# A decoder layer in fp32: the attention's output projection as three fp32r products, and another order of the last batch's work

## The chip, the cores and the metric

The kernel runs on one core of a Trainium2 chip. The metric is the device time of one execution in microseconds. It is taken as the median of several runs.

## What is computed

Four batches (B = 4) of 256 tokens with 256 channels go through one layer of three parts. Each part ends in a residual and a layer norm. Cut to what matters:

```python
q, k, v = (x @ Wq), (x @ Wk), (x @ Wv)             # 16 heads of 128; q and k RMS-normed
attn = softmax(q @ k.T / sqrt(128) - slope_h * dist, causal)
y = rmsnorm(attn @ v) * subln_w
x = layernorm(x + y.reshape(B, T, 2048) @ Wproj)   # the output projection, 2048 -> 256
e = (ctx @ xWq.T + bq) @ (ctx @ xWk.T + bk).T
x = layernorm(x + x @ softmax(e))                   # mixes the 256 channels
xq = quantise(x, per token, 127 steps); gate, up, down weights ternary
h = sigmoid(xq @ gate.T) * (xq @ up.T)              # 1024 wide, quantised again per token
x = layernorm(x + quantise(h) @ down.T)
```

All of it is fp32, apart from the last part, whose quantised integers are exact in bf16. x, Wq, Wk and Wv are each split into a rounded part of type fp32r ("hi") and the rest of it, fp32r too ("lo"). A product of two such numbers is summed from three matmuls: hi by hi, hi by lo, and lo by hi.

## The kernel before, in words

The program is written engine by engine, with semaphores set by hand, and each engine does its instructions in the order written. A batch has 16 heads, so there are 64 heads. One loop of 68 steps is a pipeline of depth 4 over them. In step n the PE queue (lines 565 to 585) holds, in this order:

- `qkv(n, 0)` (line 504): token tile 0 of head n, six fp32r matmuls of 384 columns
- `turn_qk(n-1)` (line 514): four fp32 transposes; `turn_p(n-2)` (line 521): three
- the first side slot; then `qkv(n, 1)`
- `scores(n-1)` (lines 526, 527) and `values(n-2)` (lines 533 to 535), in fp32
- `project(n-4)` (line 546): for each of the two token tiles one fp32 matmul of `yT` by `wp[:, h]`, 256 columns wide, summed over the 16 heads in bank 7
- `turn_y(n-3)` (line 554): two transposes; then the second side slot

A side slot (`slots`, lines 49 to 79) may hold a job of the rest of the layer: the cross attention of the same batch, or the second and third part of the layer for the batch before. All such jobs write PSUM bank 6.

The other engines in step n:

- ScalarE (lines 724 to 770): two exponentials of head n-2 (731, 732), `yT` of head n-4 from PSUM to SBUF with a scale (737), the squares and the copy of v for tile 0 (709, 713), the copies of q, k and P (749, 750, 755), the squares for tile 1, side jobs, and the squares of y (770).
- VectorE (lines 1055 to 1132): the norm of tile 1 of head n-1 (823), sums of y of head n-3 (1067), for the first 13 steps a split of a head's weights (1003, 1008), layer-norm work, sums of tile 0 (829), y of head n-3 (1089), norm of tile 0, sums of tile 1, the scores of head n-1 (1105), then side jobs.
- GpSimd (lines 366 to 389): the power -1/2 of those sums (371, 376), in the first 13 steps two pieces of `w_lo` (326), and small columns.

The last batch's second and third part have no loop left to hide in. After step 67 they are done tile by tile (`for t in range(TT)`), and batch 2's last matmuls, add and norm are held back and placed between. On VectorE these are lines 1125 to 1170: the held hidden layer of batch 2 is rounded and clipped (894, 895), the projection is taken (851), x1 is normed (863), the cross product is added (1141), centred (899), its largest value found (900), and it is quantised (909 to 917). Then the hidden layer goes by halves of 512 (890, 926, 929 to 932), is rounded (938, with 790 on ScalarE) and clipped (939, 942). PE's share is lines 594 to 645, ScalarE's 772 to 803, GpSimd's 390 to 394.

A helper orders instructions of one engine that depend on each other:

```python
def link(ins):
    chain[0] += 1
    ins.then_inc(s_dve, 1)
    dve.wait_ge(s_dve, chain[0])
```

`res`, `x1`, `x2`, `hid`, `fin`, `xq`, `hT` are views of `ff_raw`, the memory of the raw feed-forward weights, and are shared by all batches. `w_lo` lies over `w_raw`.

Of the kernel before, what the change touches and what calls it, by code (L numbers as in the profile page):

```python
# [1 line left out]

# [12 lines left out]
P = 128  # L15
EPS = 1e-5
# [5 lines left out]
QKS_BANK, PT_BANK, Y_BANK, YT_BANK, SIDE_BANK, SUM_BANK = 2, 3, 4, 5, 6, 7  # L22


def decoder_kernel(nc, x, ctx_in, wq, wk, wv, wproj, q_rms, k_rms, subln, xwq, xbq, xwk, xbk,
# [56 lines left out]
    with ctx:  # L82
# [11 lines left out]
        with nc.sbuf_tensor("w_raw", [P, H, KC * W3], F32) as w_raw:  # L94
# [3 lines left out]
        wp = sb("wp", [P, H, C])  # L98
        yT = sb("yT", [P, 2, T])
# [17 lines left out]
        prob = sb("prob", [P, 3 * P])  # L117
        pT = sb("pT", [P, 3 * P])
        v_sb = sb("v_sb", [P, 4, TT, VW])
# [7 lines left out]
        qcT = sb("qcT", [P, T])  # L127
        kcT = sb("kcT", [P, T])
        attn_raw = sb("attn_raw", [P, TT, T])
        attn = sb("attn", [P, 2, TT, T])  # L130
# [34 lines left out]
        gate_up_scale = sb("gate_up_scale", [P, TT, 2])  # L165
        round_col = sb("round_col", [P, 1])
# [17 lines left out]
            "constants_set", "w_hi_set", "w_lo_set", "dist_set", "vecs_scaled"))  # L184
        s_w0hi, s_w1hi = sem("w_head0_hi_set"), sem("w_head1_hi_set")
# [24 lines left out]
        s_th2, s_hT2, s_dn2 = (sem(n) for n in ("held_hidden_turned", "held_hT_copied", "held_down_done"))  # L210
        s_xc, s_x2, s_hT_dve = (sem(n) for n in ("last_x2_centred", "last_x2_scaled", "last_hT_copied_by_vector"))
# [26 lines left out]
        def _(sp):  # L238
# [25 lines left out]
            def load_wp(i):  # L264
                sp.dma_start(wp[:, 4 * i:4 * i + 4, :], wp_d[:, 4 * i:4 * i + 4, :]).then_inc(s_wp[i], 16)
# [38 lines left out]
        def _(pool):  # L304
# [61 lines left out]
            for n in range(STEPS + 3):  # L366
# [5 lines left out]
                if n < STEPS:  # L372
                    for t in range(TT):
# [3 lines left out]
                        if n + 3 < H:  # L377
                            split_lo(n + 3, t)
# [813 lines left out]
```

## Time and profile before

| | |
|---|---|
| median of 3 runs | 432.35 us (432.35 to 432.9) |
| the profiled execution | 433.11 us |
| its span in the profile | 431.3 us |
| PE / VectorE / ScalarE / GpSimd busy | 400.9 / 298.5 / 281.4 / 181.0 us |
| mean granted TensorE clock | 0.971 of 2.4 GHz |
| stage up to 20 us | loads, first heads |
| 20 to about 387 us | the loop of 64 heads |
| about 387 to 398.6 us | the loop drains |
| from 398.6 us | second and third part of the last batch |

The span is that of the instructions; the execution's own time is 1.8 us longer. A busy time is the union of the records of an engine. PE's records hold the time that a result takes through the array, so the time between two starts, and not the length of a record, is what a matmul costs in a row of them.

### The profile page before, as it was taken

What the parts mean: (1) busy time and instruction counts of PE and PEld (TensorE: products, weight loads), DVE (VectorE), ACT (ScalarE), POOL (GpSimd) and SP (SyncE); (2) the same over time, 40 slices, a digit from 0 to 9 for tenths busy, and PEclk for the clock granted to TensorE, in tenths of its full rate; (3) what the DMA queues carried; (4) which work ended last, traced back from release to release, by engine and by line L of the source; (5) the groups of instructions that cost most, each with busy time, mean ns of one, the idle gap of its engine ahead of it and who ended that gap; (6) DMA issues with size and microseconds to landing.
All of it is one profiled execution on the core that took longest, in us unless ns stands there. A gap on an engine that the chain in (4) does not pass through costs nothing.

```text
span 431.3 us, 8778 instructions
## 1 busy us (share of the span) xinstructions
PE 400.9 (93%) x2610; PEld 368.1 (85%) x2620; DVE 298.5 (69%) x933; ACT 281.4 (65%) x800; POOL 181.0 (42%) x283
## 2 busy tenths in 40 slices
PE   4699999999999999999999999999999999997653
PEld 3599998999999998999999998999999999986421
DVE  4678878876777577767576576667575676675695
ACT  3287876677777587667857587667757577764251
POOL 3676766633334333335435333335344343322301
PEclk9699999999999999999999999999999999999885
DMA  7999200000000000000002000000000000000000
GB/s 192 276 296 325 71 1 2 2 0 15 0 26 2 2 2 2 0 2 0 2 2 61 2 0 3 0 2 2 1 2 26 0 2 1 2 2 2 1 24 24
DMA packets 21662, 14.84 MB, mean 34 GB/s; under 512 B 1648, under 2 KB 21360, under 8 KB 21616
## 3 DMA queue, kind: packets, MB, share of 16 engines
q1 hardware_dynamic: 20800, 13.90, 11.1%
q8 instruction: 21, 0.34, 0.3%
q10 hardware_dynamic: 816, 0.39, 0.3%
q14 instruction: 25, 0.20, 0.1%
HBM read 13.24 MB, written 1.05 MB: 33 GB/s over the span
## 4 chain that ended last, share of the span: by engine, by line
PE 87%; DVE 7%; issue 2%; POOL 1%; DMA 1%; ACT 1%; POOLq 0%; DVEq 0%; ACTq 0%
PE ps L504 31%; PE ps L546 12%; PE ps L514 7%; PE ps L527 7%; PE ps L521 5%; PE ps L526 3%; PE ps L533 3%; PE ps L535 3%; PE ps L534 3%; PE ps L554 3%; PE ps L467 2%; PE ps L455 1%; DMA x_sb<-in_x 1%; PE ps L477 1%; PE ps L416 1%
## 5 line engine op out<-in xcount | busy, mean ns | idle before, releaser
L376 POOL TENSOR_TENSOR qk_rstd<-qk_sum,minus_half 128x2 f32<-128x2 f32 x128 | 92.8, 725 | 115.3 <-DVE qk_sum L829 114.7
L504 PE MATMUL ps<-w_hi,xT_hi 128*128 128x384 f32 x256 | 101.7, 399 | 4.1 <-DVE qk_n L823 2.3
L829 DVE TENSOR_REDUCE qk_sum<-sq 128x2 f32<-128x258 f32 x128 | 53.9, 421 | 74.2 <-ACT sq L709 70.2
L709 ACT ACTIVATE sq<-ps 128x256 f32<-128x256 f32 x128 | 49.3, 386 | 74.2 <-PE ps L504 74.1
L504 PE MATMUL ps<-w_hi,xT_lo 128*128 128x384 f32 x256 | 87.2, 342 | 0.0
L371 POOL TENSOR_TENSOR y_rstd<-y_sum,minus_half 128x2 f32<-128x2 f32 x64 | 47.3, 740 | 94.8 <-DVE y_sum L1067 93.2
L504 PE MATMUL ps<-w_lo,xT_hi 128*128 128x384 f32 x256 | 86.9, 341 | 0.0
L823 DVE TENSOR_TENSOR qk_n<-ps,qk_rstd 128x256 f32<-128x256 f32 x128 | 53.9, 421 | 33.4 <-POOL qk_rstd L376 33.2
L546 PE MATMUL ps<-wp,yT 128*128 128x256 f32 x256 | 66.0, 380 | 1.1 <-ACT yT L737 1.1
L504 PEld LDWEIGHTS ps<-w_hi,xT_hi 128*128 128x128 f32 x256 | 49.3, 193 | 8.0 <-issue 2.5
L504 PEld LDWEIGHTS ps<-w_lo,xT_hi 128*128 128x128 f32 x256 | 49.2, 193 | 1.3 <-POOL w_lo L331 0.3
L770 ACT ACTIVATE sqy<-ps 128x258 f32<-128x258 f32 x64 | 24.9, 388 | 37.5 <-PE ps L535 37.5
L504 PEld LDWEIGHTS ps<-w_hi,xT_lo 128*128 128x128 f32 x256 | 49.1, 192 | 0.0
L546 PEld LDWEIGHTS ps<-wp,yT 128*128 128x128 f32 x256 | 43.6, 190 | 4.9 <-ACT yT L737 1.6
L514 PE MATMUL ps<-ident,qk_n 128*128 128x128 f32 x256 | 39.1, 276 | 3.3 <-issue 1.9
L1105 DVE CUSTOM_DVE_ANT_0 score<-ps,dist 128x128 f32<-128x128 f32 (+1 forms) x128 | 40.1, 351 | 1.5 <-PE ps L527 1.5
L527 PE MATMUL ps<-kT,qT 128*128 128x256 f32 x128 | 38.7, 384 | 0.0
L514 PEld LDWEIGHTS ps<-ident,qk_n 128*128 128x128 f32 x256 | 31.0, 141 | 8.4 <-issue 6.4
L713 ACT COPY v_sb<-ps 128x128 f32<-128x128 f32 x128 | 33.5, 262 | 0.0
L749 ACT ACTIVATE qT<-ps,q_scale 128x256 f32<-128x256 f32 x64 | 30.7, 479 | 4.2 <-PE ps L514 4.0
L737 ACT ACTIVATE yT<-ps,vecs 128x256 f32<-128x256 f32 x64 | 30.4, 474 | 2.7 <-PE ps L554 2.1
L732 ACT ACTIVATE prob<-score,neg_max 128x256 f32<-128x256 f32 x64 | 32.1, 502 | 0.0
(184 smaller groups left out, 780.1 us busy)
## 6 DMA issues: line engine op xcount, KB each, us to landing
wp<-in_L_attn_Wproj SPq DMA_DIRECT2D x4, 512.0 KB, 5.9
x_sb<-in_x SPq DMA_DIRECT2D x4, 256.0 KB, 3.4
ff_raw<-in_L_ffn_w_gate SPq DMA_DIRECT2D x1, 1024.0 KB, 7.9
ff_raw<-in_L_ffn_w_up SPq DMA_DIRECT2D x1, 1024.0 KB, 10.4
w_raw<-in_L_attn_Wq SPq DMA_DIRECT2D x4, 256.0 KB, 7.1
w_raw<-in_L_attn_Wk SPq DMA_DIRECT2D x4, 256.0 KB, 5.7
w_raw<-in_L_attn_Wv SPq DMA_DIRECT2D x4, 256.0 KB, 5.6
ff_raw<-in_L_ffn_w_down SPq DMA_DIRECT2D x1, 1024.0 KB, 8.1
```

The lines of the kernel that those rows point to most:

```text
L371: pool.tensor_tensor(y_rstd[:], y_sum[:], minus_half[:], ALU.pow).then_inc(s_ry, 1)
L376: pool.tensor_tensor(qk_rstd[:, t, :], qk_sum[:, t, :], minus_half[:], ALU.pow).then_inc(s_rs[t], 1)
L504: last = pe.matmul(ps[:, t, 0:W3], xa[:, b % 2, k, tok], wa[:, h, k * W3:(k + 1) * W3], start=(i == 0), stop=(i == len(parts) - 1))
L514: last = pe.transpose(dst[:, t * P:(t + 1) * P], qk_n[:, t, a, :], ident[:])
L527: pe.matmul(ps_s[:, S1], qT[:, P:T], kT[:], start=True, stop=True).then_inc(s_s, 1)
L546: last = pe.matmul(total[:, t * C:(t + 1) * C], yT[:, n % 2, t * P:(t + 1) * P], wp[:, h, :], start=(h == 0 and t == 0), stop=(h == H - 1) ...
L709: act.activation(sq[:, t, :, 0:D], ps[:, t, 0:2 * D].rearrange("p (a d) -> p a d", a=2), ACT.Square).then_inc(s_sq[t], 1)
L713: act.copy(v_sb[:, n % 4, t, 0:D], ps[:, t, 2 * D:3 * D]).then_inc(s_v[t], 1)
L732: act.activation(prob[:, S1], score[:, S1], ACT.Exp, bias=neg_max[:, 1:2], scale=-1.0).then_inc(s_p, 1)
L823: dve.tensor_tensor(qk_n[:, t], ps[:, t, 0:2 * D].rearrange("p (a d) -> p a d", a=2), r, ALU.mult).then_inc(s_qkn[t], 1)
L829: dve.tensor_reduce(qk_sum[:, t, :], sq[:, t], AX.X, ALU.add).then_inc(s_ss[t], 1)
L1105: last = dve.tensor_tensor_reduce(score[:, cols], ps_s[:, cols], dist[:, cols], slope, 3e38, ALU.add, ALU.min, neg_max[:, t:t + 1])
```

## The change

- The projection: `wp` (fp32) becomes `wp_hi` and `wp_lo`, and `yT` becomes `yT_hi` and `yT_lo`, all fp32r. Two fp32 matmuls of 256 columns per head become six fp32r matmuls. `yT_hi` is made by ScalarE where `yT` was; VectorE makes `yT_lo` in a new instruction per head, and the projection waits for that. For each of the first 16 heads ScalarE copies `wp_hi` and GpSimd subtracts `wp_lo`.
- Memory: `prob` is now `score`; `v_sb` has three buffers, not four; `attn` one, not two; `qcT` and `kcT` lie in `attn_raw`; `hq` of the early batches lies over `x1` and `x1T`.
- The last batch's tiles lie in `w_raw` and no longer in `ff_raw`. Its two tiles go through VectorE's queue interleaved, with waits by count (`mark`) in place of `link`. The `gate_up_scale`, `up_127` and `down_scale` columns go from VectorE to GpSimd; the rounding of batch 2's held hidden layer, the rounding of tile 0's first half and batch 2's last norm go to ScalarE (the norm with a bias column from GpSimd). `keep_busy` is called with a count of 0.

The diff, cut:

```diff
-        wp = sb("wp", [P, H, C])
-        yT = sb("yT", [P, 2, T])
+        wp_hi = sb("wp_hi", [P, H, C], F32R)
+        with nc.sbuf_tensor("wp_raw", [P, H, C], F32) as wp_raw:
+            pass
+        wp_lo = sb("wp_lo", [P, H, C], F32R)
+        yT_hi = sb("yT_hi", [P, 2, T], F32R)
+        yT_lo = sb("yT_lo", [P, 2, T], F32R)
...
-        prob = sb("prob", [P, 3 * P])
+        prob = score
...
@@ gpsimd, step n, after the power of tile t
+                        if t == 1 and 0 <= n - 3 < H:
+                            h = n - 3
+                            pool.wait_ge(s_wphi, h + 1)
+                            pool.tensor_tensor(wp_lo[:, h], wp_raw[:, h], wp_hi[:, h].bitcast(F32),
+                                               ALU.subtract).then_inc(s_wplo, 1)
...
@@ tensor, project(n)
-                pe.wait_ge(s_yT, n + 1)
+                pe.wait_ge(s_yTlo, n + 1)
...
                 for t in range(TT):
-                    last = pe.matmul(total[:, t * C:(t + 1) * C], yT[:, n % 2, t * P:(t + 1) * P], wp[:, h, :],
-                                     start=(h == 0 and t == 0), stop=(h == H - 1), skip_group_check=True)
+                    for i, (ya, wa) in enumerate(((yT_hi, wp_hi), (yT_hi, wp_lo), (yT_lo, wp_hi))):
+                        last = pe.matmul(total[:, t * C:(t + 1) * C], ya[:, n % 2, t * P:(t + 1) * P], wa[:, h, :],
+                                         start=(h == 0 and t == 0 and i == 0), stop=(h == H - 1 and i == 2),
+                                         skip_group_check=True)
...
@@ scalar, step n, after the first side job
+                if 0 <= n - 3 < H:
+                    h = n - 3
+                    if h % 4 == 0:
+                        act.wait_ge(s_wp[h // 4], 16)
+                    act.copy(wp_hi[:, h], wp_raw[:, h]).then_inc(s_wphi, 1)
...
+                if n in (STEPS + 2, STEPS + 3):
+                    t = n - STEPS - 2
+                    act.wait_ge(s_hs, LAST)
+                    act.activation(early.hid[:, t], early.hid[:, t], ACT.Identity, scale=h_inv[:, t:t + 1],
+                                   bias=round_col[:]).then_inc(s_hr2, 1)
...
@@ vector, step n, ahead of sums(n, 0)
+                if 0 <= n - 4 < STEPS:
+                    m = n - 4
+                    dve.wait_ge(s_yT, m + 1)
+                    dve.scalar_tensor_tensor(out=yT_lo[:, m % 2], in0=ps_yT, scalar=sub_scale,
+                                             in1=yT_hi[:, m % 2].bitcast(F32), op0=ALU.mult,
+                                             op1=ALU.subtract).then_inc(s_yTlo, 1)
...
-                if n == STEPS + 2:
+                if n == STEPS + 3:
                     for t in range(TT):
-                        quantise_hidden_at_once(LAST - 1, t)
+                        dve.wait_ge(s_hr2, t + 1)
+                        clip(early.hq[:, t], early.hid[:, t]).then_inc(s_hq, 1)
...
@@ vector, after the loop
+            added0 = add_cross(0)
+            dve.wait_ge(s_dve, added0)
+            stats0 = take_stats(late.res, one(0))
+            added1 = add_cross(1)
+            aggregate(1, one(0), stats0)
...
+            clip_x2(0, rounded0)
+            rounded1 = round_x2(1, by1)
 
             wait(dve, s_out, 16 * (LAST - 1))
             dve.wait_ge(s_dn2, 1)
+            take_down(LAST - 1, 0, side[:, 0:C])
+            clip_x2(1, rounded1)
+            down1 = mark(take_down(LAST - 1, 1, side[:, C:2 * C]))
...
+            made00 = hidden_half(0, 0)
+            made01 = hidden_half(0, 1)
+            largest_half(0, 0, made00)
+            found0 = largest_half(0, 1, made01)
+            made10 = hidden_half(1, 0)
+            found0 = largest_hidden(0, found0)
+            made11 = hidden_half(1, 1)
+            scale_of_hidden(0, found0)
+            hidden_quantiser(0)
+            largest_half(1, 0, made10)
+            found1 = largest_half(1, 1, made11)
+            clip_half(0, 0, 1)
+            found1 = largest_hidden(1, found1)
+            clip_half(0, 1, 2)
+            scale_of_hidden(1, found1)
+            hidden_quantiser(1)
...
@@ tensor, after the loop
+            turn_hidden(0, 0)
+            turn_hidden(0, 1)
+            down_half(0, 0)
+            turn_hidden(1, 0)
+            down_half(0, 1)
+            turn_hidden(1, 1)
+            down_half(1, 0)
+            down_half(1, 1)
```

## Rows read from the trace of the kernel before

**Rows 1.** The page's busy times, with shares of the span and instruction counts.

```profile
PE 400.9 (93%) x2610; PEld 368.1 (85%) x2620; DVE 298.5 (69%) x933; ACT 281.4 (65%) x800; POOL 181.0 (42%) x283
```

**Rows 2.** Busy time by stretch: length, each engine's busy (count), PE clock, DMA, GB/s.

```profile
17.00:19.00 2.00, 2.00 (x9) 2.00 (x8) 1.17 (x3) 0.73 (x2) 1.18 (x2) 0.50 1.08 311
...
200.00:300.00 100.00, 99.58 (x671) 93.38 (x672) 66.70 (x213) 69.43 (x201) 40.61 (x62) 1.00 0.03 8
```

**Rows 3.** The chain that ended last, one step: start us, length us, what.

```profile
383.08 1.04 PE ps L504 x6
...
385.45 0.86 PE ps L546 x4
```

**Rows 4.** Timeline, PE at full clock: start us, length us of the merged records.

```profile
202.13 0.61 PE L473 MATMUL ps<-ident,hq 128*128 128x128 bf16 x8
202.55 0.42 PE L504 MATMUL ps<-w_hi,xT_hi 128*128 128x384 f32 x1
202.81 0.34 PE L504 MATMUL ps<-w_lo,xT_hi 128*128 128x384 f32 x1
```

**Rows 5.** Timeline, weight loads (PEld) of the first two of those fp32r matmuls.

```profile
202.52 0.19 PEld L504 LDWEIGHTS ps<-w_hi,xT_hi 128*128 128x128 f32 x1
202.63 0.19 PEld L504 LDWEIGHTS ps<-w_lo,xT_hi 128*128 128x128 f32 x1
```

**Rows 6.** Timeline, PE at half clock, two matmuls one after the other.

```profile
17.66 0.52 PE L504 MATMUL ps<-w_lo,xT_hi 128*128 128x384 f32 x1
17.98 0.52 PE L504 MATMUL ps<-w_hi,xT_lo 128*128 128x384 f32 x1
```

**Rows 7.** Groups by line and shape: count, busy us, mean ns, idle before.

```profile
L1089 DVE TENSOR_TENSOR y_n<-ps,y_rstd 128x256 f32<-128x256 f32 x64 | 26.7, 417 | 3.7 <-POOL y_rstd L371 3.6
L951 DVE SCALAR_TENSOR_TENSOR ff_raw<-ps,down_scale,ff_raw 128x256 f32<-128x256 f32 x8 | 3.6, 479 | 0.7 <-PE ps L643 0.7
L764 ACT ACTIVATE hq<-ff_raw 128x1024 bf16<-128x1024 f32 x3 | 3.2, 1070 | 0.0
L326 POOL TENSOR_TENSOR w_lo<-w_raw,w_hi 128x256 fp32r<-128x256 f32 x28 | 21.4, 766 | 2.7 <-DVE w_hi L1003 2.7
```

**Rows 8.** Timeline of one step, ScalarE and VectorE: in brackets idle before, and releaser.

```profile
380.44 0.47 ACT L737 ACTIVATE yT<-ps,vecs 128x256 f32<-128x256 f32 x1
...
380.99 0.41 DVE L1067 TENSOR_REDUCE y_sum<-sqy 128x2 f32<-128x258 f32 x1
...
382.35 0.42 DVE L829 TENSOR_REDUCE qk_sum<-sq 128x2 f32<-128x258 f32 x1 [0.95 <-ACT sq L709]
```

**Rows 9.** Timeline of a step after a long side job: the norm and its reader.

```profile
200.78 0.42 DVE L823 TENSOR_TENSOR qk_n<-ps,qk_rstd 128x256 f32<-128x256 f32 x1
...
201.37 0.60 PE L514 MATMUL ps<-ident,qk_n 128*128 128x128 f32 x4
```

**Rows 10.** Timeline where the loop drains, steps 66 and 67.

```profile
395.45 1.13 PE L546 MATMUL ps<-wp,yT 128*128 128x256 f32 x4 [0.57 <-ACT yT L737]
...
396.83 0.47 ACT L737 ACTIVATE yT<-ps,vecs 128x256 f32<-128x256 f32 x1 [1.44 <-PE ps L554]
...
398.60 0.42 DVE L851 TENSOR_TENSOR ff_raw<-ps,x_sb 128x256 f32<-128x256 f32 x1
```

**Rows 11.** Busy time by stretch after the loop, columns as in rows 2.

```profile
404.15:411.23 7.08, 4.91 (x26) 3.19 (x27) 6.44 (x24) 0.76 (x2) 1.78 (x4) 0.84 0.00 1
411.23:423.73 12.50, 6.33 (x34) 3.08 (x32) 11.87 (x33) 5.73 (x10) 0.89 (x2) 0.72 0.06 21
```

**Rows 12.** Timeline after the loop: VectorE's order, and the last matmuls.

```profile
413.78 0.69 DVE L926 TENSOR_REDUCE h_parts<-ff_raw 128x1 f32<-128x512 f32 x1
...
414.39 0.68 DVE L890 SCALAR_TENSOR_TENSOR ff_raw<-ff_raw,ps 128x512 f32<-128x512 f32 x1
...
416.71 0.73 DVE L863 TENSOR_SCALAR ff_raw<-ff_raw,mean_var,ln_rstd 128x256 f32<-128x256 f32 x2
...
424.61 1.89 PE L643 MATMUL ps<-wdT,ff_raw 128*128 128x256 bf16 x8 [0.22 <-ACT ff_raw L793]
```

More of the change, by code:

```diff
@@ L1 @@
 from contextlib import ExitStack
+from typing import NamedTuple
 import numpy as np
@@ L585, in _, with keep_busy @@
                 slot(n, 1)
+            FILL = (0, 0, 0, 0)
+            def keep_busy(bank, count):
+                for _ in range(count):
+                    pe.matmul(ps[:, bank, :], ident16[:], wgT[:, 0, 0:BANK], start=True, stop=True)
             def bank16(i):
@@ L591, in _, with turn_hidden, down_half @@
             HALF = FC // 2
+            def turn_hidden(t, half):
+                pe.wait_ge(s_hq, 2 * LAST + 2 * t + half + 1)
+                for f in range(HALF):
+                    of = (half * HALF + f) * P
+                    last = pe.transpose(bank16(4 * t + 2 * half)[:, f * P:(f + 1) * P], late.hq[:, t, of:of + P],
+                                        ident16[:])
+                last.then_inc(s_th, 1)
+            def down_half(t, half):
+                if t == 1 and half == 1:
+                    pe.wait_ge(s_hT_dve, 1)
+                else:
+                    pe.wait_ge(s_hT, 2 * t + half + 1)
+                for f in range(half * HALF, (half + 1) * HALF):
+                    last = pe.matmul(ps[:, 4 * t + 1, 0:C], late.hT[:, t, f, :], wdT[:, f, :], start=(f == 0),
+                                     stop=(f == FC - 1))
+                if half == 1:
+                    last.then_inc(s_dn, 1)
             pe.wait_ge(s_side_out, len(JOB))
@@ L1138, in _, with one, add_cross @@
                 norm_x1(LAST, slice(t, t + 1))
-            for t in range(TT):
+            def one(t):
+                return slice(t, t + 1)
+            def add_cross(t):
                 dve.wait_ge(s_xm, t + 1)
-                link(dve.tensor_tensor(res[:, t], ps[:, 4 * t + 1, 0:T], x1[:, t], ALU.add))
-                take_stats(res, slice(t, t + 1))
-                aggregate(1, slice(t, t + 1))
+                return mark(dve.tensor_tensor(late.res[:, t], ps[:, 4 * t + 1, 0:T], late.x1[:, t], ALU.add))
@@ L1144, in _, with centre, largest @@
+            def centre(t):
                 dve.wait_ge(s_mv[1], tiles_done(LAST, t))
-                centre_x2(t)
-            for t in range(TT):
-                quantise_centred(t)
+                return mark(dve.tensor_scalar(late.res[:, t], late.res[:, t], mean_var[:, 1, t, 0:1], None, ALU.subtract))
+            def largest(t, done):
+                dve.wait_ge(s_dve, done)
+                dve.tensor_reduce(x_most[:, one(t)], late.res[:, t], AX.X, ALU.max,
+                                  apply_absolute_value=True).then_inc(s_xc, 1)
@@ new lines, in _ @@
+            aggregate(1, one(0), stats0)
+            dve.wait_ge(s_dve, added1)
+            stats1 = take_stats(late.res, one(1))
+            centred0 = centre(0)
+            aggregate(1, one(1), stats1)
+            largest(0, centred0)
+            centred1 = centre(1)
+            scale_of_x2(0)
+            largest(1, centred1)
+            over0 = over_scale(0)
+            scale_of_x2(1)
+            by0 = quantiser(0, over0)
+            over1 = over_scale(1)
+            rounded0 = round_x2(0, by0)
@@ L1149, in _ @@
+            by1 = quantiser(1, over1)
+            clip_x2(0, rounded0)
+            rounded1 = round_x2(1, by1)
             wait(dve, s_out, 16 * (LAST - 1))
             dve.wait_ge(s_dn2, 1)
-            for t in range(TT):
-                last = take_down(LAST - 1, t, side[:, t * C:(t + 1) * C])
-            link(last)
-            take_stats(fin, BOTH)
-            aggregate(2, BOTH)
-            hidden_halves(0)
-            normed(2, LAST - 1, BOTH, fin, fin).then_inc(s_fin, 1)
-            quantise_halves(0)
```

359 lines of the change are left out of this document (204 added, 155 removed).

## The prediction

> **What bounds the kernel now.** I read the busy times first, then PE's share by stretch, the chain, and last the timelines of single steps. PE is busy 93% of the span and no other engine over 69% [rows 1]. From 200 to 300 us, which stands for the whole loop, PE is busy 99.58 of 100 us at a granted clock of 1.00, which is the 2.4 GHz level, while VectorE is busy 66.7 us [rows 2]. In a step the chain runs from PE group to PE group: 1.04 us for the six fp32r matmuls of one token tile, 0.86 us for the four instructions of the projection [rows 3]. So in the loop the time is the sum of PE's groups, and what leaves PE leaves the time. After the loop it is another program. From 404.15 to 423.73 us VectorE is busy 6.44 of 7.08 and 11.87 of 12.50 us, PE about half of it [rows 11]: VectorE's queue sets the end there, apart from the last few us.
>
> **The projection on PE.** It costs 0.86 us per head, four instructions of 0.215 [rows 3] (each of the two fp32 matmuls stands as two instructions). It becomes six fp32r matmuls of 256 columns, a form that the trace doesn't hold. The nearest is the fp32r matmul of 384 columns, 1.04 / 6 = 0.173 us apart [rows 3]. At half clock (0.50, the 1.2 GHz level [rows 2]) two of them start 0.32 us apart [rows 6], 0.833 ns a column, so at full clock the columns alone need 0.160 and 0.013 is left over. With 256 columns the bounds are these. From below: columns alone, 0.107. If the rest grows with the columns, 0.115; if it is fixed, 0.120. From above: the 0.173 stays, because something other than the columns sets it. Is the weight load that something? It is recorded with 0.19 us, longer than the spacing. But behind eight short bf16 transposes the first load starts at 202.52, the second at 202.63 [rows 5], and a load starts when the matmul before it does: so the first matmul really started 0.11 after its load. The record agrees: this matmul is 0.42 long and not 0.34, by 0.08 of waiting [rows 4]. A load thus needs 0.11 us, about the 256 columns' own time, and can lie under them. I take 0.118, between the two middle values: 6 x 0.118 = 0.71, a gain of 0.15 us per head. The last three projections wait for data in the drain, so 61 heads count: 61 x 0.15 = **9.2 us gained**. The ends: 0.107 gives 0.22 x 61 = 13.4 gained; 0.173 gives 1.04, 0.18 x 61 = 11.0 lost. Between them, loads that don't quite hide, at 0.130, give 4.9 gained.
>
> The Trainium skill ("TensorE: Matmul & The Clock Gate", Back-to-back issue gap) gives N / 2.4 + 2.5 ns between matmuls, so as an estimate 0.109 us each and a gain of 12.5 us. By that rule 384 columns would stand at 0.1625, and the trace has 0.173, so I stay with the row.
>
> **What hides the added work in the loop.** VectorE gets one instruction per head, 256 columns from PSUM with a column scale. Its bounds are 0.42 (line 1089) and 0.48 us (line 951) [rows 7]; 64 x 0.45 = 29 us more, to 328 of some 420 us. It stands ahead of the sums of tile 0. In an ordinary step its input, the copy by ScalarE, is there at 380.91; the instruction before it ends at 381.40; and the sums wait 0.95 us for ScalarE's squares, until 382.35 [rows 8]. So it runs in a gap, at no cost. The projection that now waits for it comes at about the end of the step, over 2 us later. If the gap is full, sums of tile 0 and all behind them come up to 0.45 us later. The tight places are steps with a long side job: there the norm ends at 201.20, and its reader on PE starts at 201.37 [rows 9]. With a shorter projection PE reaches that point 0.15 us sooner. For some ten such steps at up to 0.15 I give back 0.5 us in all (0 to 1.5). ScalarE's copy of `wp_hi` lies ahead of a wait for PE and costs nothing. GpSimd's subtraction costs 0.77 us [rows 7] in 16 steps that already hold two such pieces and three powers; it delays the y powers, whose reader stands behind tile 0's sums on VectorE. Nothing, or 0.2 us in each of 13 steps if not: up to 2.6. The single `attn`, three `v_sb` and `prob` in `score` wait only for PE work that stands earlier in PE's own queue: nothing, and at most part of the 1.5 above.
>
> **The drain, steps 66 and 67.** Here each link counts, and the new one is in it twice. Now: ScalarE's copy of head 62 frees the projection at 395.45; the copy of head 63 is 396.83 to 397.30; VectorE rounds and clips the held hidden layer in four instructions until 398.6, then takes the projection at 398.60 [rows 10]. Then: `yT_lo` of 62 ends near 395.8, and the norm of y for head 63 behind it on VectorE starts 0.3 later; the copy of 63 ends near 397.55, `yT_lo` near 398.0, and the projection is summed by 399.0. VectorE has only two clips left, but the second waits for ScalarE's second rounding, which starts behind the copy at 397.55 and lasts 1.07 (line 764, the same size [rows 7]): clip from 398.8 to 399.5. The projection is taken at about 399.5, **0.85 us lost** (0.4 to 1.3). What was to leave the path is held by another engine.
>
> **The two tiles of the last batch.** An instruction with a link behind it costs its length and 0.04; without a link the next starts before it is over, 413.78 to 414.39, 0.61 for a length of 0.69 [rows 12]. So interleaving gives 0.08 + 0.04 per 256- or 512-wide instruction. First stretch, from the cross product to the rounding of tile 1, on the old clock: per tile 0.34 (add) + 0.37 + 0.15 (moments) + 0.28 (centre) + 0.34 (largest) + 4 small ones, 0.57, + 0.28 (round), 2.33, and 0.22 for one clip: 4.9 in place of 7.08 less the clip 0.3 and the two columns' 0.5 (now GpSimd's). So it ends at 409.0. Batch 2's add and moments and the second clip take 2.1, and 0.25 goes on waiting for the first tanh, since both tiles' transposes now stand ahead of tile 0's gate matmuls: 411.35. Then until the quantiser of tile 1: eight 512-wide instructions at 0.61, two clips at 0.36, small ones 2 x 0.8: 7.2, so 418.55; before it was 422.3. Gone from VectorE are batch 2's norm, 0.73 [rows 12], one rounding and two columns. From there to the last down matmul PE needed 4.2; now one group of `down_half(0, 1)`, 4 x 0.213 at half clock, and ScalarE's copy of tile 0 lie ahead of tile 1's second half: 4.85, so 423.4 in place of 426.55. **3.15 us gained** (1 to 5). With the drain's loss the end gains 2.3 (0 to 4.5).
>
> **Sum:** -9.2 + 0.5 + 0.85 - 3.15 = -11.0 us. The profiled execution took 433.11 with a span of 431.3, so it becomes 422.1 with a span of 420.3; the median before is 432.35, 0.76 below the profiled one, and I predict 432.35 - 11.0 = 421.35, **421.4 us**.
>
> **Rivals.**
>
> (1) The forecast: PE's groups get shorter and the rest hides. For it: VectorE's 0.95 us gap and PE at 99.6%. Chance 0.76, between 415.5 and 429.
>
> (2) Slower: an fp32r matmul costs 0.173 us whatever its columns, since its load, 0.19 in the record, starts with the matmul before and is waited for. Place: the projection; price +11.0 in the loop, +0.5 - 2.3 for the rest, 441.6. It decides from 0.143 us per matmul on, where six cost what the four did, and from 0.15 on the end's gain is used up too. For it: spacing and load record are near each other at both clocks (0.32 against 0.33 us). Against it: 0.32 is also exactly the columns at half clock, and the 0.11 of rows 5. Chance 0.08. The Trainium skill (same page, "The mechanism", what overlaps and what doesn't) says that a weight load overlaps a matmul in flight only when their row groups differ; here they are the same. As a mechanism of this kernel that is 0.107 + 0.11 = 0.217 each, 1.30 per head, +27 us, 457. But by it 384 columns would be 0.27 apart, and they are 0.173 [rows 3]. Chance 0.01.
>
> (3) The projection's gain is taken back: PE gets to its waits earlier and finds the chain of ScalarE, VectorE and GpSimd not ready, since VectorE got 0.45 us a step. Only the end gains: 430.0. For it: the 0.17 us of rows 9. Against it: ordinary steps have 0.95 us of slack. Chance 0.09.
>
> (4) The order by hand at the end gains nothing but the loop does: 432.35 - 8.7 = 423.7. Inside the range, counted in (1).
>
> (5) The change doesn't do what it says: the 256-column form runs at the fp32 rate, six of 0.215 each, 1.29 per head: +26 us, 456. Against it: the 384-column form doesn't. Chance 0.02. The remaining 0.04 is for small mixtures around no change.
>
> **How the numbers follow.** Best ends: 13.4 + 4.5 - 0.85 is 17, to 415.5. For the other end, loads at 0.130 (4.9), 1.5 given back in the loop and nothing at the end: 429. To hold part of (3) I go to 430.5; what is left out is (2), (5) and a rest. A measurement of this kernel can tell about 0.2%, 0.9 us, from no change. Faster by more than that: (1), (3) and a part of the rest, 0.86. Same: 0.03. Slower: 0.11.
>
> **What would show it.** Right: in the chain, project's group of six near 0.71 us in place of 0.86, with starts 0.12 apart; PE still over 99% busy in the loop; the step 0.15 shorter; VectorE's idle before the sums of tile 0 shorter by 0.45; the take of the projection later by 0.85 counted from the last qkv group; VectorE's stretch from the cross product to the quantiser of tile 1 at about 14.4 us in place of 18.1. Wrong: starts 0.17 apart would make (2) true; new idle of PE ahead of the transposes of q and k with VectorE's norm as releaser would make (3) true.

## The result and the profile after

The changed kernel takes 429.54 us (median of 7 runs, 427.68 to 431.31). The kernel before took 432.35 us in 7 runs on the same chip (431.84 to 433.39). The ratio is 0.9924, interval 0.9907 to 0.9941. It is faster by 2.8 us in the medians and by 3.3 in the ratio, where 11.0 was forecast. The changed kernel's runs spread over 3.6 us, the ones of before over 1.6. The profiled execution is the fastest of the seven, 427.68 us with a span of 425.9, so the traces differ by more than the medians do.

The page's busy times of the changed kernel, against [rows 1]:

```profile
PE 392.1 (92%) x2738; PEld 366.2 (86%) x2748; DVE 323.0 (76%) x986; ACT 286.1 (67%) x821; POOL 193.7 (45%) x307
```

PE lost 8.8 us of busy time, but the span only 5.4. The chain that ended last (start, length, what), one step of it, against [rows 3]:

```profile
377.55 0.72 PE ps L606 x6
```

The projection takes 0.72 us in place of 0.86. The timeline of three matmuls of one projection at full clock (start us, length us) gives their spacing, and the one of their weight loads answers to [rows 5]:

```profile
200.58 0.28 PE L606 MATMUL ps<-wp_lo,yT_hi 128*128 128x256 f32 x1
200.70 0.28 PE L606 MATMUL ps<-wp_hi,yT_lo 128*128 128x256 f32 x1
200.82 0.28 PE L606 MATMUL ps<-wp_hi,yT_hi 128*128 128x256 f32 x1
```

```profile
200.46 0.19 PEld L606 LDWEIGHTS ps<-wp_lo,yT_hi 128*128 128x128 f32 x1
200.58 0.19 PEld L606 LDWEIGHTS ps<-wp_hi,yT_lo 128*128 128x128 f32 x1
```

The matmuls start 0.12 us apart, and each load starts with the matmul before it: loads of 0.19 us in the record do lie under 256 columns. So the matmuls do what was forecast. Now the busy time by stretch (length, then PE, PEld, VectorE, ScalarE, GpSimd busy with their counts, PE clock, DMA, GB/s). Before, in the first batch:

```profile
60.00:80.00 20.00, 19.47 (x134) 18.43 (x133) 17.13 (x57) 13.81 (x42) 13.34 (x18) 1.00 0.01 2
80.00:100.00 20.00, 19.86 (x140) 18.69 (x139) 14.73 (x47) 15.09 (x44) 8.57 (x12) 1.00 0.00 1
```

After, the same stretches and the one that stands for the loop in [rows 2]:

```profile
60.00:80.00 20.00, 18.32 (x133) 17.40 (x131) 18.08 (x54) 14.77 (x45) 14.35 (x19) 1.00 0.01 2
80.00:100.00 20.00, 18.12 (x135) 17.05 (x135) 16.67 (x49) 13.88 (x42) 11.15 (x17) 1.00 0.01 2
...
200.00:300.00 100.00, 99.34 (x715) 94.69 (x717) 74.88 (x236) 68.96 (x203) 42.11 (x65) 1.00 0.03 8
```

In the middle of the run PE is as full as before. In the first batch it is not: from 60 to 100 us it is busy 36.44 us where it was 39.33. The prediction argued from one stretch, 200 to 300 us, and took it for the whole loop.

How far the changed kernel is ahead of the old one, at the start of the q, k and v group of a step (worked out from the PE records of one execution of each kernel, in us, the kernel less the one before; the other columns are kernels that come below):

```text
step   before at   after     e1      e4      e2      e3      e5      e9     e12
 8       51.92     -0.40   -0.70   -0.70   -0.51   -1.05   -0.12   -0.27   -0.51
12       75.54     +0.55   -0.70   -1.15   -0.55   -0.97   +0.11   -0.54   -0.10
16       98.21     +2.47   -0.66   -1.44   -0.47   +0.26   -0.20   -1.26   +1.11
20      121.49     +2.65   -0.63   -1.99   -1.02   +0.45   -0.75   -1.86   +1.56
40      243.08     +0.68   -0.60   -4.11   -2.98   -1.68   -2.79   -4.82   +1.58
62      374.35     -1.76   -0.62   -6.60   -5.44   -4.16   -5.22   -7.25   +1.56
```

The first steps differ by chance (at step 4, up to where e5 and e7 are alike, they stand at +0.05 and -0.62), so what counts is how a column moves from step 8 on. Between steps 8 and 20 the changed kernel loses 3 us. Only from there on does it win, by 4.4 us over 42 steps. The waits of PE from 15 to 120 us (waited for: us in total, times, longest us) say where. Before:

```profile
PE ps L514 <- DVE qk_n L823: 1.1, 1, 1.1
PE ps L514 <- issue: 0.5, 1, 0.5
```

After:

```profile
PE ps L573 <- issue: 4.0, 6, 1.6
PE ps L573 <- DVE qk_n L932: 0.9, 2, 0.7
```

Both lines are the transposes of q and k, which read VectorE's norm of tile 1: 1.6 us of waiting became 4.9. "issue" here is a wait whose releaser the profile does not name; the timeline of step 13 does (in brackets PE's idle time):

```profile
81.77 0.81 POOL L361 TENSOR_TENSOR w_lo<-w_raw,w_hi 128x256 fp32r<-128x256 f32 x1
82.02 0.84 DVE L1088 TENSOR_SCALAR ff_raw<-ff_raw 128x512 f32<-128x512 f32 x1
82.54 0.91 POOL L417 TENSOR_TENSOR wp_lo<-wp_raw,wp_hi 128x256 fp32r<-128x256 f32 x1
82.89 0.83 DVE L1092 TENSOR_SCALAR ff_q<-ff_raw 128x512 bf16<-128x512 f32 x1
83.65 0.41 DVE L932 TENSOR_TENSOR qk_n<-ps,qk_rstd 128x256 f32<-128x256 f32 x1
84.16 0.63 PE L573 MATMUL ps<-ident,qk_n 128*128 128x128 f32 x4 [1.30 <-issue]
```

PE's transposes start 0.1 us behind the end of VectorE's norm. Ahead of the norm, VectorE makes ternary weights in three passes over `ff_raw`. The first (line 1087, 0.48 us) stands just before these rows; the second and third are the rows of 0.84 and 0.83 us. GpSimd is subtracting during both of them.

### The profile page after: what moved, and what is told of

It reads as the page before. It is cut to its first block, busy times and chain, and to the rows that moved or that the text cites. A ratio compares the mean times of both kernels' runs of the same rounds, so it can differ in the third digit from the quotient of the medians.

```text
span 425.9 us, 9094 instructions
## 1 busy us (share of the span) xinstructions
PE 392.1 (92%) x2738; PEld 366.2 (86%) x2748; DVE 323.0 (76%) x986; ACT 286.1 (67%) x821; POOL 193.7 (45%) x307
## 4 chain that ended last, share of the span: by engine, by line
PE 88%; DVE 4%; issue 3%; POOL 2%; ACT 1%; DMA 1%; POOLq 0%; DVEq 0%; ACTq 0%
PE ps L563 31%; PE ps L606 10%; PE ps L573 8%; PE ps L586 7%; PE ps L580 5%; PE ps L592 3%; PE ps L585 3%; PE ps L593 3%; PE ps L594 3%; PE ps L615 3%; PE ps L526 2%; PE ps L514 1%; PE ps L536 1%; PE ps L475 1%; PE ps L478 1%
## 5 line engine op out<-in xcount | busy, mean ns | idle before, releaser
L606 PE MATMUL ps<-wp_hi,yT_hi 128*128 128x256 f32 x128 | 41.5, 324 | 2.2 <-DVE yT_lo L1147 2.2
L573 PEld LDWEIGHTS ps<-ident,qk_n 128*128 128x128 f32 x256 | 29.9, 142 | 15.4 <-issue 13.6
L606 PE MATMUL ps<-wp_hi,yT_lo 128*128 128x256 f32 x128 | 36.0, 281 | 0.0
L606 PE MATMUL ps<-wp_lo,yT_hi 128*128 128x256 f32 x128 | 36.0, 281 | 0.0
L1147 DVE SCALAR_TENSOR_TENSOR yT_lo<-ps,vecs,yT_hi 128x256 fp32r<-128x256 f32 x64 | 30.6, 478 | 4.6 <-ACT yT_hi L822 4.4
```

The lines of the kernel that those rows point to most:

```text
L573: last = pe.transpose(dst[:, t * P:(t + 1) * P], qk_n[:, t, a, :], ident[:])
L606: last = pe.matmul(total[:, t * C:(t + 1) * C], ya[:, n % 2, t * P:(t + 1) * P], wa[:, h, :], start=(h == 0 and t == 0 and i == 0), stop=( ...
```

## The experiments

Two things were open: which of the two new instructions gives the gain back (`wp_lo` on GpSimd in 16 steps, or `yT_lo` on VectorE in 64), and whether it acts by its time in its engine's queue or by slowing VectorE beside it. In this table "ratio" is to the kernel before on the same chip.

```text
kernel                         median us   ratio    interval
changed                          429.54    0.9924   0.9907 to 0.9941
e1  fp32 projection              430.71    0.9954   0.9938 to 0.9970
e2  no wp_lo                     424.59    0.9812   0.9793 to 0.9832
e3  no yT_lo                     427.40    0.9879   0.9849 to 0.9909
e4  neither                      423.88    0.9798   0.9783 to 0.9812
e5  wp_lo earlier in the step    426.34    0.9838   0.9825 to 0.9852
e6  a power in wp_lo's place     426.23    0.9831   0.9814 to 0.9849
e7  e5, yT_lo later              428.35    0.9886   0.9865 to 0.9907
e8  e7, first pass on ScalarE    425.14    0.9817   0.9804 to 0.9831
e9  e8, yT_lo where it was       424.54    0.9816   0.9797 to 0.9835
e10 e9, matmuls to fill waits    422.11    0.9759   0.9741 to 0.9777
e11 changed, matmuls to fill     427.48    0.9880   0.9861 to 0.9898
e12 before, with a subtraction   434.29    1.0042   1.0026 to 1.0059
```

### The parts apart: e1 to e4

**e1** is the changed kernel with the old projection; the memory plan and the order at the end stay changed.

```diff
-((yT_hi, wp_hi), (yT_hi, wp_lo), (yT_lo, wp_hi))
+((yT_hi, wp_raw),)          # yT_hi in fp32; no yT_lo, wp_hi, wp_lo
```

> The changed kernel, with the projection as it was: two fp32 matmuls, no yT_lo, no wp_hi, no wp_lo. It keeps the new memory and the new order of the end. If the end gained what the two traces show from the last q, k, v group on (3.7 us), it takes 432.35 - 3.7 = 428.7. If that was the clock of one execution (1.00 at 400 to 410 us after, 0.83 before) and the order itself gave the 2.3 us of the prediction or less, 430.1 or above. If the drain lost nothing here, since yT_lo is gone, it may go to 427.5.

Measured: 430.71 us against 432.79, 0.9954. In the loop it keeps a constant lead of 0.6 to 0.7 us from step 8 on, so `prob` in `score`, three `v_sb` for four and the single `attn` cost nothing. From the last q, k and v group to the end it takes 46.0 us where before took 48.6. The end alone is thus worth up to 2 us; if the lead of 0.6 us from before step 8 is in every execution, which one profile can't tell, it is 1.4.

**e2** leaves out the subtraction; in place of `yT_hi` by `wp_lo` it adds `yT_hi` by `wp_hi` a second time.

```diff
-pool.tensor_tensor(wp_lo[:, h], wp_raw[:, h], wp_hi[:, h].bitcast(F32), ALU.subtract)
-((yT_hi, wp_hi), (yT_hi, wp_lo), (yT_lo, wp_hi))
+((yT_hi, wp_hi), (yT_hi, wp_hi), (yT_lo, wp_hi))
```

> The changed kernel without GpSimd's 16 subtractions for wp_lo; the matmul that read it reads wp_hi, so this term of the projection is left out and PE's work is the same. Theory A (VectorE's queue is full in the first batch by its own new instruction): same as the changed kernel, 429.5. Theory B (GpSimd's subtraction lengthens VectorE's instructions beside it, 0.84 in place of 0.43 us): most of the 5.6 us of new waits in the first batch go, 424.5. Both together: 427.

**e3** leaves out `yT_lo` in the same manner.

```diff
-dve.scalar_tensor_tensor(out=yT_lo[:, m % 2], ...)
-((yT_hi, wp_hi), (yT_hi, wp_lo), (yT_lo, wp_hi))
+((yT_hi, wp_hi), (yT_hi, wp_lo), (yT_hi, wp_hi))
```

> The changed kernel without VectorE's instruction for yT_lo; the matmul that read it reads yT_hi, so this term is left out and PE's work is the same. Theory A: the 5.6 us of waits in the first batch, the 1.4 us in later steps and 0.8 in the drain go: 421.7. Theory B: only the 1.4 and 0.8 go: 427.3. Both together: 424.5.

**e4** leaves out both; PE still does six fp32r matmuls. ScalarE still copies `wp_hi`.

> Both left out, with PE's work as in the changed kernel. Under A and under B this is what PE's shorter groups and the end give without a cost elsewhere: 429.5 - 7.8 = 421.7, near the prediction of 421.4. If it stays above 425, the lost time is neither VectorE's nor GpSimd's new work but something of the memory changes or ScalarE's copies.

Measured: e2 424.59, e3 427.40, e4 423.88 us. From e4 the steps are these. `yT_lo` alone costs 0.7 us (e2). `wp_lo` alone costs 3.5 (e3). Both together cost 5.7 (the changed kernel), so each is dearer beside the other. The sixteen subtractions, on top of `yT_lo`, cost 4.9 us: about 0.3 each, in an engine that is busy 45% of the span. The projection's shorter groups are worth 6.8 (e1 to e4).

The step table has the same order without the end of the kernel, whose time varies from run to run. At step 62, from e4, `yT_lo` costs 1.2 us, `wp_lo` 2.4 and both 4.8; the subtractions on top of `yT_lo` cost 3.7, nearly all of it between steps 8 and 20. The other 1.2 of the 4.9 lies outside the loop or in the scatter of the medians. e4 was expected at 421.7 and is 2.2 us above it, though under its bound of 425: that part of the lost time belongs to neither instruction, and the section on the prediction finds most of it.

The step of e2 that answers to step 13 of the changed kernel, as a timeline:

```profile
80.08 0.81 POOL L361 TENSOR_TENSOR w_lo<-w_raw,w_hi 128x256 fp32r<-128x256 f32 x1
80.33 0.85 DVE L1083 TENSOR_SCALAR ff_raw<-ff_raw 128x512 f32<-128x512 f32 x1
81.21 0.43 DVE L1087 TENSOR_SCALAR ff_q<-ff_raw 128x512 bf16<-128x512 f32 x1
81.56 0.42 DVE L927 TENSOR_TENSOR qk_n<-ps,qk_rstd 128x256 f32<-128x256 f32 x1
82.07 0.63 PE L568 MATMUL ps<-ident,qk_n 128*128 128x128 f32 x4 [0.64 <-issue]
```

Here the second pass lies beside the last `w_lo` and lasts 0.85 us too; the third, with GpSimd free, lasts 0.43. PE waits 0.64 in place of 1.30 us. VectorE's second and third pass from 30 to 200 us, and its rounding of a head's q, k and v weights (`w_hi`), by shape (count, busy us, mean ns, idle before), in e2:

```profile
L1083 DVE TENSOR_SCALAR ff_raw<-ff_raw 128x512 f32<-128x512 f32 x12 | 5.6, 463 | 0.4
L1087 DVE TENSOR_SCALAR ff_q<-ff_raw 128x512 bf16<-128x512 f32 x12 | 5.1, 427 | 0.7 <-PE ps L499 0.3
L1061 DVE CAST w_hi<-w_raw 128x768 fp32r<-128x768 f32 x9 | 4.9, 549 | 0.0
```

In the changed kernel:

```profile
L1088 DVE TENSOR_SCALAR ff_raw<-ff_raw 128x512 f32<-128x512 f32 x12 | 8.4, 703 | 0.4
L1092 DVE TENSOR_SCALAR ff_q<-ff_raw 128x512 bf16<-128x512 f32 x12 | 5.5, 461 | 0.7 <-PE ps L504 0.3
L1066 DVE CAST w_hi<-w_raw 128x768 fp32r<-128x768 f32 x9 | 6.9, 769 | 0.0
```

The same 24 passes take 13.9 in place of 10.7 us, and the nine roundings 6.9 in place of 4.9: 5.2 us more, in the queue that PE's transposes wait for. Of the roundings four are long (0.85 to 1.12 us), those beside a subtraction of `wp_lo`; the others stay at 0.55. The Trainium skill ("SBUF — State Buffer", SBUF: two separate sides) says that VectorE and GpSimd share a pair of ports as an exclusive lock, which holds one engine's instruction up while the other's runs, for some forms of VectorE's. The trace agrees: the pass took about 0.84 us beside a subtraction of 0.8 to 0.9 us, and 0.43 without one.

### Traffic or queue: e5 to e7

**e5** leaves nothing out. GpSimd subtracts behind the power of tile 0, no longer behind that of tile 1, and ScalarE copies `wp_hi` one step earlier. **e7** is e5 with `yT_lo` moved behind tile 0's norm. **e6** is the changed kernel with a power of two columns where the subtraction was; it leaves out `wp_lo`, as e2 does.

```diff
# e5, GpSimd, then ScalarE
-if t == 1 and 0 <= n - 3 < H:
+if t == 0 and 0 <= n - 3 < H:
-h = n - 3
+h = n - 2
# e6
-pool.tensor_tensor(wp_lo[:, h], wp_raw[:, h], wp_hi[:, h].bitcast(F32), ALU.subtract)
+pool.tensor_tensor(idle[:, 2 * h:2 * h + 2], ones[:, 0:2], minus_half[:], ALU.pow)
# e7, on top of e5, VectorE: the block of yT_lo stood ahead of sums(n, 0)
 norm(n, 0)
+dve.scalar_tensor_tensor(out=yT_lo[:, m % 2], ...)
 sums(n, 1)
```

> GpSimd's subtraction for wp_lo stands behind the power of tile 0, no longer behind that of tile 1; ScalarE's copy is made one step sooner. Nothing is left out. Beside it VectorE then does norms, sums and scores (from PSUM, or reductions), not the three passes over the raw feed-forward weights. If only those passes are lengthened: near the kernel without the subtraction, 425.0 to 426. If every instruction of VectorE is, or if the length of GpSimd's queue is what counts: 429, no change.

> In the place of GpSimd's subtraction of 128x256 elements (0.77 us) stands a power of 128x2 elements (about 0.7 us), so GpSimd's queue is as long and its memory traffic is nearly none; the term of wp_lo is left out of the projection. Theory B1 (the two engines get in each other's way at the memory): 424.6, as without the subtraction. Theory B2 (GpSimd's queue makes the powers late, and VectorE waits for them): 429, as changed.

> As e5, and VectorE's instruction for yT_lo stands behind the norm of tile 0, ahead of the sums of tile 1, no longer ahead of the sums of tile 0. Nothing is left out. What yT_lo still costs (0.7 us between the kernels without the subtraction) comes from steps that begin with VectorE behind; the later place has free time in them: 0.5 to 1 below e5, 424.5 to 425. In the drain the norm of y goes ahead of yT_lo, which may give 0.3 more.

Measured: e5 426.34, e6 426.23, e7 428.35 us. The second pass by shape, 60 to 110 us, changed, then e5, then e6:

```profile
L1088 DVE TENSOR_SCALAR ff_raw<-ff_raw 128x512 f32<-128x512 f32 x6 | 5.0, 841 | 0.2
```

```profile
L1088 DVE TENSOR_SCALAR ff_raw<-ff_raw 128x512 f32<-128x512 f32 x7 | 3.4, 487 | 0.2
```

```profile
L1089 DVE TENSOR_SCALAR ff_raw<-ff_raw 128x512 f32<-128x512 f32 x7 | 3.4, 487 | 0.2
```

In e6 GpSimd has as many instructions to do, about as long (0.75 us a power, 0.78 a subtraction, on average from 20 to 110 us), and moves almost no data. It gets back from 0.9924 to 0.9831, 4.0 us of the 4.9. At most 0.8 is left for the length of GpSimd's queue; the intervals of e6 and e2 overlap, and in the loop the two differ by 0.4 us. In e5 the same subtraction lies elsewhere in the step, VectorE's passes and roundings are short again (0.55 us for all nine roundings), and 3.7 us (0.9924 to 0.9838) come back with the whole computation done. So it is the place beside those instructions that costs, and not the work. e7 was a miss: it is 2 us slower than e5. In the loop it is only 0.5 us behind e5 at step 62 (-4.73 against -5.22), and its end is 47.2 us long against 46.5. Its three slowest runs (428.35 to 429.99 us) are those with a mean granted clock of 0.973 or 0.974; e5's runs had 0.976 to 0.986. So part of the 2 us goes with the clock; how much stays open.

### Against the kernel before: e12

**e12** is the kernel before with one GpSimd subtraction of the same size in steps 3 to 18, into memory that nothing reads.

```diff
+if t == 1 and 0 <= n - 3 < H:
+    pool.tensor_tensor(idle[:, n % 2], wp[:, 0], wp[:, 1], ALU.subtract)
```

> The kernel before with one more GpSimd subtraction of 128x256 fp32 elements in each of steps 3 to 18, behind the power of tile 1, into memory that nobody reads. PE's work is unchanged. Theory B1 (GpSimd's traffic lengthens VectorE's passes over the raw weights, and VectorE's queue then holds up PE): slower, but by less than the 4.9 us in the changed kernel, since VectorE has 0.48 us a step more to spare here: 1 to 2.5 us, 434 to 435.5. If the lost time needs something else of the change: 432.8.

Measured: 434.29 us against 432.45, 1.0042 (1.0026 to 1.0059), slower by 1.8. That is inside the 1 to 2.5 us expected of the traffic. The second pass there, 60 to 110 us, and in the kernel before:

```profile
L1030 DVE TENSOR_SCALAR ff_raw<-ff_raw 128x512 f32<-128x512 f32 x6 | 5.0, 840 | 0.2
```

```profile
L1025 DVE TENSOR_SCALAR ff_raw<-ff_raw 128x512 f32<-128x512 f32 x7 | 3.4, 487 | 0.2
```

VectorE is slowed as much as in the changed kernel (840 against 841 ns), and by the step table the loss is complete at step 20. From step 8 to 20 the subtractions cost 2.1 us in the old loop (e12), 2.8 in e3's (against e4), whose projection is 0.14 us a step shorter, and 3.6 in the changed one (against e2), which holds `yT_lo` too; in the medians it is 1.8, 3.5 and 4.9. The less slack VectorE's queue has, the more of the same slowing reaches PE.

### What to do about it: e8 to e11

**e8** is e7 with the first pass over the raw weights (line 1087, the one that subtractions lengthen least) on ScalarE. **e9** is e8 with `yT_lo` back in its place, ahead of tile 0's sums. Neither leaves anything out.

```diff
# e8, VectorE, then ScalarE in FF_STEPS
-link(dve.tensor_scalar(raw, raw, w_inv[:, i:i + 1], ROUND, ALU.mult, ALU.add))
+dve.wait_ge(s_wr, FF_DONE[i, quarter])
+act.activation(raw, raw, ACT.Identity, scale=w_inv[:, i:i + 1], bias=round_col[:]).then_inc(s_wr, 1)
```

> As e7, and ScalarE does the first of the three passes over the raw feed-forward weights (12 times 0.5 us less for VectorE, 0.7 us more for ScalarE). Nothing is left out. If VectorE's queue is still what PE waits for in the first batch, the waits that the kernel before has there too (1.0 us in steps 11 and 13) go: 423 to 424. If ScalarE becomes late for the copies of q and k, no gain or a loss against e7.

> As e8, but yT_lo back in its place ahead of the sums of tile 0. Nothing is left out. e7 was slower than e5 by the place of yT_lo alone (0.5 us in steps 12, 28 and 59 of the loop, the rest at the end). If that was the place and not the clock at the end: 0.5 to 2 us below e8, 423.5 to 424.5. If it was the clock's luck: as e8, 425.

Measured: e8 425.14, 0.9817; e9 424.54, 0.9816. e8 missed its 423 to 424 us. The pass on ScalarE is worth 1 us over e5 by the ratios (0.9838 to 0.9816), with intervals that overlap, and 2.0 in the loop of the traces (-7.25 against -5.22 at step 62). The place of `yT_lo` makes no difference between the ratios of these two, and 0.3 us in their loops, which speaks against it as the cause of e7's 2 us. At step 62 e9 is further ahead than e4 without either part (-6.60).

**e10** is e9, and **e11** the changed kernel, each with `keep_busy` given counts: 7, 6 and 14 bf16 matmuls of 512 columns, whose result nothing reads, ahead of PE's waits for x1, for the quantised x2 and for the quantised hidden layer of tile 0, after the loop.

```diff
-FILL = (0, 0, 0, 0)
+FILL = (7, 6, 14, 0)
```

> As e9, with 7, 6, 14 and 0 matmuls of 512 columns into a free bank where PE waits for VectorE after the loop (1.5, 1.3 and 3.0 us of PE's idle time of 2.3, 2.0 and 4.0). Nothing is left out. In e8's profile the clock fell to the 1.2 GHz level five times after step 62, and the end from the last q, k, v group on took 48.5 us; in the changed kernel's profile it fell twice and took 45.1. If the clock is what makes the difference and these matmuls hold it up: 1.5 to 3 us below e9 and a narrower spread. If they only stand in PE's way: slower than e9 by up to 1 us.

> The changed kernel with the same filling matmuls and nothing else. Its seven runs lay between 427.68 and 431.31. If the spread is the clock at the end, they come to 427 to 428 with a spread of 1 us; if it is something else, 429.5 with the old spread.

Measured: e10 422.11 (421.60 to 422.79), e11 427.48 (426.71 to 428.00). So the filling gives 2.4 us on e9, and 2.1 on the changed kernel, whose runs (four) now spread over 1.3 us and not 3.6 (seven). The mean granted clock of the runs went with it: 0.989 to 0.995 in e10 for 0.974 to 0.979 in e9, and 0.986 to 0.992 in e11 for 0.970 to 0.993. The windows of the end show what changed, the granted clock being the third number from the last. Before, changed, e8, e9 and e10, in this order:

```profile
376.00:432.00 56.00, 36.51 (x214) 26.82 (x214) 38.06 (x111) 22.94 (x52) 12.79 (x28) 0.83 0.03 10
```

```profile
376.00:432.00 56.00, 31.10 (x215) 23.90 (x215) 33.76 (x103) 25.46 (x52) 13.45 (x34) 0.93 0.03 10
```

```profile
391.00:394.40 3.40, 2.77 (x19) 2.68 (x20) 2.80 (x7) 1.40 (x3) 0.00 (x0) 0.52 0.03 5
376.00:432.00 56.00, 30.29 (x180) 21.92 (x179) 30.28 (x92) 21.70 (x42) 11.85 (x32) 0.84 0.03 10
```

```profile
376.00:432.00 56.00, 28.01 (x179) 19.87 (x177) 29.85 (x90) 21.27 (x41) 11.49 (x32) 0.88 0.03 10
```

```profile
376.00:432.00 56.00, 31.16 (x203) 20.94 (x201) 29.36 (x90) 21.30 (x40) 11.38 (x31) 0.94 0.03 10
```

In e8 the clock fell to the 1.2 GHz level five times between 391 and 421.8 us, the first time in the drain, where PE had waited 1.61 and 1.08 us for `yT_lo`. From the last q, k and v group its end took 48.5 us where e2 to e4, with the same instructions after the loop, took 45.6 to 46.1. e10's clock there is 0.94 and its end 45.4 us. e10 is the best version here: 0.9759 (0.9741 to 0.9777), 10.3 us under the kernel before and some 7 under the changed one.

## Why the prediction was wrong

- **The projection on PE**: 0.72 us per head for the forecast 0.71, starts 0.12 apart for 0.118. Right per head. As a sum, 61 x 0.15 = 9.2 was forecast; e1 to e4 show 6.8 in the medians, and 6.7 in the loop from step 4 on. The step that failed is that every one of the 61 heads gains. Set beside e1's, e4's steps 4 to 62 fall in two kinds: 48 are shorter, by 0.14 us on average, and eleven (11, 13, 22, 25, 27, 33, 36, 40, 43, 52 and 56) by 0.03 us or less. In ten of these eleven the transposes of q and k start 0.10 to 0.16 us later behind their q, k and v group than in e1; in step 22 it is these (0.04) and a side job's transposes together. What the projection gave, the wait in front of the transposes took. That is 1.6 us; the rest of the missing 2.4 is 0.14 us a step for 0.15, and two heads fewer. Step 25, before and changed:

```profile
153.07 0.42 DVE L823 TENSOR_TENSOR qk_n<-ps,qk_rstd 128x256 f32<-128x256 f32 x1
153.59 0.63 PE L514 MATMUL ps<-ident,qk_n 128*128 128x128 f32 x4 [0.32 <-issue]
```

```profile
155.38 0.42 DVE L932 TENSOR_TENSOR qk_n<-ps,qk_rstd 128x256 f32<-128x256 f32 x1
155.90 0.63 PE L573 MATMUL ps<-ident,qk_n 128*128 128x128 f32 x4 [0.47 <-issue]
```

  The idle time is 0.15 us longer; the step is as long as it was. The prediction named such steps and had their number right ("some ten such steps at up to 0.15"), but took a third of that price, 0.5 us with a bound of 1.5, where nearly all of it was paid: 1.6.
- **`yT_lo` hides in VectorE's 0.95 us gap**: nearly right. Alone it costs 0.7 us (e4 to e2; 1.2 in the loop of the traces). With the subtraction beside it, it costs 2.1 (e3 to changed). That it does run in the gap, the groups by shape (count, busy us, mean ns, idle before) show: the new instruction, and the sums of q and k of both tiles, whose idle time for ScalarE's squares was 70.2 us before. It fell by 27.3 us, against 30.6 of new work:

```profile
L1147 DVE SCALAR_TENSOR_TENSOR yT_lo<-ps,vecs,yT_hi 128x256 fp32r<-128x256 f32 x64 | 30.6, 478 | 4.6 <-ACT yT_hi L822 4.4
L938 DVE TENSOR_REDUCE qk_sum<-sq 128x2 f32<-128x258 f32 x128 | 53.6, 419 | 43.4 <-ACT sq L795 42.9
```

- **GpSimd's subtraction, "nothing, or 0.2 us in each of 13 steps if not: up to 2.6"**: this is the step that failed most. It cost 4.9 us (e2 to changed; 3.7 in the loop of the traces), outside its own bound. The prediction followed what waits for GpSimd's result, the y powers, and not what its traffic does to an instruction that waits for nothing of it. The rows that would have said so were in the old trace, in the timeline of step 13:

```profile
80.25 0.81 POOL L326 TENSOR_TENSOR w_lo<-w_raw,w_hi 128x256 fp32r<-128x256 f32 x1
80.50 0.84 DVE L1025 TENSOR_SCALAR ff_raw<-ff_raw 128x512 f32<-128x512 f32 x1
81.38 0.43 DVE L1029 TENSOR_SCALAR ff_q<-ff_raw 128x512 bf16<-128x512 f32 x1
```

  One of twelve second passes there met the last `w_lo` and took 0.84 us, the other eleven 0.43. The change puts a subtraction beside the eight of them that fall in steps 10 to 18.
- **The drain**: from the last q, k and v group (380.80, before 382.73) to the take of the projection it took 16.7 us in place of 15.9, 0.87 more for the forecast 0.85, and the chain is the one forecast. These are rows of the changed kernel's drain:

```profile
394.06 0.39 PE L606 MATMUL ps<-wp_hi,yT_hi 128*128 128x256 f32 x1 [1.08 <-DVE yT_lo L1147]
395.30 0.47 ACT L822 ACTIVATE yT_hi<-ps,vecs 128x256 fp32r<-128x256 f32 x1 [0.68 <-PE ps L615]
395.67 1.23 ACT L865 ACTIVATE ff_raw<-ff_raw,round_col,h_inv 128x1024 f32<-128x1024 f32 x1
395.80 0.48 DVE L1147 SCALAR_TENSOR_TENSOR yT_lo<-ps,vecs,yT_hi 128x256 fp32r<-128x256 f32 x1 [1.47 <-ACT yT_hi L822]
396.93 0.69 DVE L1011 TENSOR_SCALAR ff_raw<-ff_raw 128x1024 bf16<-128x1024 f32 x1
397.54 0.42 DVE L961 TENSOR_TENSOR w_raw<-ps,x_sb 128x256 f32<-128x256 f32 x1
```

  The new link is in the path twice, and the second clip starts 0.03 us behind the end of ScalarE's second rounding (396.90), with the take behind it. How much each holds is less even than it looks. Without `yT_lo` (e3 and e4) the same stretch is 16.1 us, so the new link is 0.7 of the 0.87. The first clip (396.20, 0.69) was over at 396.89, so ScalarE held the second one up by about 0.1 us only.
- **The end**: from the cross product (402.68, before 404.15) to the quantiser of tile 1 (416.78, before 422.28) 14.1 us for the forecast 14.4, before 18.1. The order by hand does what was forecast, but the size is in part luck of the clock, which was granted in full until 416.3 us in this execution. The same stretch took 14.1 us in e2, e10 and e11 too, 14.3 to 15.1 in e1, e3 to e7 and e9, and 16.3 in e8. In the medians e1, which has no `yT_lo` in the drain, gained 2.1 us where 3.15 was forecast for this part. The rest may have gone with the clock at the end; e1 was not run with the filling, so this is not shown.
- **The rivals**: (2) and (5) are refuted by the spacing of 0.12 us. (3), the gain taken back, is what happened in good part: 5.7 us for the two new instructions and 1.6 in steps that did not get shorter, 7.3 us where 1.35 was forecast (0.5 in the loop and 0.85 in the drain). Its releaser was right, VectorE's norm ahead of the transposes of q and k. Its cause was not: mostly it is not that VectorE got 0.45 us a step, but that GpSimd slowed it in one batch.
- **The sum**: -6.8 for the projection, -2.1 for the end and +5.7 for the two new instructions give -3.2 us, against -2.8 and -3.3 measured. The forecast range reached up to 430.5 to hold part of (3), and only for that does 429.54 lie in it. At its lower end the drain's 0.85 is taken off a gain of 4.5 that already had it off; nothing hangs on that.

## What to carry to other kernels

When work goes to an engine with time to spare, read not only its queue and its readers, but also which instructions of other engines run beside it, and whether the same shape has two durations in the trace (0.43 and 0.84 us here). If the long ones lie beside another engine's work, suspect something that the two share; a move within the step may then be all but free (e5). Before counting a gain on the bounding engine times the number of steps, find the steps in which it already waits, in every stage and not in one that stands for all; those steps gain nothing. A busy share near 100% does not rule them out. After a loop whose engine falls into waits, look at the granted clock: cheap matmuls in the waits gave 2.1 and 2.4 us, and steadier runs.

## What the runs showed of the hardware that was not expected

- Beside a GpSimd subtraction of 128x256 a VectorE pass over 128x512 took 0.84 us in place of 0.43, and a rounding of 128x768 up to 1.12 in place of 0.55. The subtraction itself took 0.91 where such a piece took 0.77 on average [rows 7]. A GpSimd power of 128x2 did not lengthen the pass (e6). VectorE's norms, sums and scores kept their length: over steps 3 to 19 its instructions take 5.5 us more in the changed kernel than in e2, and 5.3 of it lie in the passes and roundings.
- A lengthened instruction ends a fixed time behind the subtraction, wherever in the subtraction it began: 0.28 or 0.29 us for every long pass of before, changed and e12 (0.68 us long where it began 0.34 us into a subtraction of 0.73, 0.84 where it began 0.25 into one of 0.81), and 0.41 or 0.42 for every long rounding of the changed kernel. That is 0.13 to 0.2 us less than the instruction takes alone. By these records it gets through its first 0.13 to 0.2 us beside the subtraction, and is held for the rest until the subtraction is over.
- PE's busy time hides short waits. In the rows above a matmul of the projection is 0.28 us long in the record while the next starts 0.12 behind it, so an engine that waits up to 0.16 us longer still looks busy. PE stood at 99.34 of 100 us from 200 to 300 us in the changed kernel, and in e4's steps 40 and 56 the records show no idle time, though the transposes start 0.10 us later than in e1.
- From the last q, k and v group to the end, kernels with the same instructions after the loop took 45.1 to 48.5 us in different profiles, by the granted clock. That scatter (3.6 us between runs of the changed kernel) is as large as the whole effect that was measured, and filling the waits took most of it away.
